# Masked cross-attention: the mask as a TensorE product ahead of the scores, the row sums as a VectorE reduction

## The reference

```python
Q = proj(q, Wq, bq); K = proj(k, Wk, bk); V = proj(v, Wv, bv)
scores = jnp.einsum('bhqd,bhkd->bhqk', Q, K) / math.sqrt(D_K)
scores = jnp.where(mask, scores, jnp.float32(-1000000000.0))   # one 128x128 mask for all
probs = jax.nn.softmax(scores, axis=-1)
attn = jnp.einsum('bhqk,bhkd->bhqd', probs, V)
```

## Time and profile before

| what | value |
|---|---|
| runs | 1013.98, 1015.27, 1017.23 us |
| span of the profiled execution, first to last instruction | 1013.6 us |
| PE busy | 946.9 us (93%) |
| PE weight loads busy | 847.0 us (84%) |
| ACT busy | 659.4 us (65%) |
| DVE busy | 635.2 us (63%) |
| POOL busy | 196.8 us (19%) |
| mean granted TensorE clock | 0.950 |
| first and last masked quad on DVE | 361.4 and 623.0 us |

### The profile page before, as it was taken

How to read it: one execution, slowest core, us unless ns; L and a number is a source line. 1 busy time by engine, 2 the same in 40 slices (tenths; PEclk the granted TensorE clock), 3 DMA queues, 4 the chain that set the end, 5 groups by cost and what they waited for, 6 DMA issues and landing times.

```text
span 1013.6 us, 19721 instructions
## 1 busy us (share of the span) xinstructions
PE 946.9 (93%) x6824; PEld 847.0 (84%) x6824; DVE 635.2 (63%) x1269; ACT 659.4 (65%) x1851; POOL 196.8 (19%) x190
## 2 busy tenths in 40 slices
PE   2899999999999899998999988999999999999997
PEld 2688989899889788877877877899999999998996
DVE  5789788788788777679787696645422342334223
ACT  3797888788888765666675576676445445444543
POOL 3112232232232432325243242100000000000000
PEclk9999999999999995788997797999999999999999
DMA  6210000000000000000100000433000000000000
GB/s 230 85 52 1 2 2 1 0 0 1 0 0 1 22 2 1 21 2 12 51 0 0 0 1 1 115 94 83 21 0 0 0 21 0 0 0 22 1 1 22
DMA packets 9998, 22.02 MB, mean 22 GB/s; under 512 B 1490, under 2 KB 1492, under 8 KB 9812
## 3 DMA queue, kind: packets, MB, share of 16 engines
q1 hardware_dynamic: 9360, 20.98, 6.5%
q10 hardware_dynamic: 580, 0.34, 0.2%
HBM read 19.21 MB, written 2.10 MB: 21 GB/s over the span
## 4 chain that ended last, share of the span: by engine, by line
PE 71%; DVE 15%; ACT 7%; issue 5%; POOL 1%; DMA 0%; DVEq 0%; ACTq 0%; POOLq 0%
PE A L414 23%; PE Y L414 21%; PE S L414 15%; PE O L414 6%; PE T L491 4%; ACT probs L695 3%; DVE nm L894 2%; DVE PT L778 2%; DVE arena L835 2%; DVE arena L915 1%; ACT arena L714 1%; DVE S L890 1%; DVE arena L922 1%; DVE xn L804 1%; ACT arena L665 1%
## 5 line engine op out<-in xcount | busy, mean ns | idle before, releaser
L778 DVE TENSOR_TENSOR PT<-probs,PT 128x512 fp32r<-128x512 f32 x128 | 88.6, 692 | 231.1 <-ACT PT L758 231.1
L414 PE MATMUL A<-XT,arena 128*128 128x512 f32 x816 | 219.1, 404 | 4.6 <-DVE arena L835 4.6
L695 ACT ACTIVATE probs<-S,nm 128x128 f32<-128x128 f32 x512 | 181.0, 369 | 47.6 <-DVE nm L894 45.9
L1111 POOL TENSOR_TENSOR probs<-probs,rinv 128x512 f32<-128x512 f32 x128 | 133.1, 1040 | 403.1 <-DVE rinv L899 403.1
L414 PEld LDWEIGHTS Y<-arena,PT 128*128 128x128 f32 x1536 | 200.3, 191 | 11.0 <-DVE PT L778 1.1
L414 PE MATMUL Y<-arena,PT 128*128 128x256 f32 x1536 | 204.0, 283 | 0.3
L414 PEld LDWEIGHTS A<-XT,arena 128*128 128x128 f32 x816 | 146.7, 192 | 35.0 <-DVE arena L835 7.3
L414 PE MATMUL O<-PT,arena 128*64 128x128 f32 (+1 forms) x1536 | 125.7, 236 | 19.9 <-DVE arena L922 9.5
L758 ACT ACTIVATE PT<-probs 128x512 fp32r<-128x512 f32 x128 | 80.8, 631 | 90.9 <-PE Y L414 90.5
L414 PEld LDWEIGHTS O<-PT,arena 128*64 128x64 f32 (+1 forms) x1536 | 112.2, 130 | 30.4 <-DVE PT L778 11.3
L414 PE MATMUL S<-arena 128*128 128x256 f32 (+1 forms) x768 | 129.3, 306 | 3.9 <-ACT probs L695 3.8
(11 more groups left out here) (96 smaller groups left out, 1065.0 us busy)
## 6 DMA issues: line engine op xcount, KB each, us to landing
wst<-in_pieces SPq DMA_DIRECT2D x52, 256.0 KB, 2.7
xs<-in_x SPq DMA_DIRECT2D x4, 512.0 KB, 4.0
craw<-in_ctxT SPq DMA_DIRECT2D x4, 512.0 KB, 3.6
out<-craw SPq DMA_DIRECT2D x4, 512.0 KB, 2.6
probs<-in_rows SPq DMA_DIRECT2D x1, 1024.0 KB, 8.1
rowc<-in_rows ACTq DMA_DIRECT2D x1, 264.0 KB
bias<-in_biases ACTq DMA_DIRECT2D x1, 37.0 KB
bkraw<-in_rows ACTq DMA_DIRECT2D x1, 2.0 KB
```

Of the source, the lines that this page charges most:

```text
L414: mm = pe.matmul(acc, lhs[a], rhs[b], start=first and i == 0, stop=last and i == 2, skip_group_check=shared)
L695: last = act.activation(probs[:, n % 4, u * P:(u + 1) * P], S[n % 2][:, u * P:(u + 1) * P], ACT.Exp, bias=nm[:, n % 4, u:u + 1], accum_out ...
L778: dve.tensor_tensor(out_, src, hi.bitcast(F32), ALU.subtract).then_inc(sem_, 1)
L1111: pool.tensor_tensor(p3, p3, rinv[:, n % 4, :].unsqueeze(2).to_broadcast([P, 4, P]), ALU.mult).then_inc(normed, 1)
```

## The change

The mask is no longer written over the scores. A constant matrix `dropped` (now fp32r, -2^60 where a key is masked, 0 elsewhere) is multiplied by an identity (`identr`, fp32r) on PE into the score bank, repeated over the four blocks by a stride of zero, and the six score matmuls accumulate onto it. On DVE the predicated copy and the wait on it are gone. In phase 1 the exponential no longer uses the accumulator; a new step `row_sum` on DVE sums the probabilities from SBUF, and the inverse waits for that sum. The hand-written order of DVE for phase 1 is another one: sum, out, inverse, probs, max instead of max, inverse, out, probs.

```diff
-MASKED = -1e9
+MASKED = -2.0 ** 60
...
-            (("max", "quad", (0, 1)), ("inverse", "quad", (1, 2)), ("out", "quad", (3, 5)),
-             ("probs", "quad", (2, 3)), ("xt1", "xt1", (0, 0)), ("residual", "residual", (4, 5)),
+            (("sum", "quad", (1, 2)), ("out", "quad", (3, 5)), ("inverse", "quad", (1, 2)),
+             ("probs", "quad", (2, 3)), ("max", "quad", (0, 1)), ("xt1", "xt1", (0, 0)), ("residual", "residual", (4, 5)),
...
                 if ph == 1:
                     pe.sem_inc(pe_gate, 1)
+                    pe.matmul(S[n % 2][:, :].rearrange("p (u c) -> p u c", u=4), identr[:, :],
+                              dropped[:, :].unsqueeze(1).to_broadcast([P, 4, P]),
+                              start=True, stop=True, skip_group_check=True)
...
                 for u in range(4):
-                    last = act.activation(probs[:, n % 4, u * P:(u + 1) * P],
-                                          S[n % 2][:, u * P:(u + 1) * P], ACT.Exp,
-                                          bias=nm[:, n % 4, u:u + 1], accum_out=rsum[:, n % 4, u:u + 1])
+                    dst, src = probs[:, n % 4, u * P:(u + 1) * P], S[n % 2][:, u * P:(u + 1) * P]
+                    if ph == 0:
+                        last = act.activation(dst, src, ACT.Exp, bias=nm[:, n % 4, u:u + 1],
+                                              accum_out=rsum[:, n % 4, u:u + 1])
+                    else:
+                        last = act.activation(dst, src, ACT.Exp, bias=nm[:, n % 4, u:u + 1])
...
-                dve.tensor_scalar(dropped[:, :], msk[:, :], 0.0, None, ALU.is_equal)
-                dve.memset(neg[:, :], MASKED)
+                dve.tensor_scalar(dropped[:, :], msk[:, :], 0.0, MASKED, ALU.is_equal, ALU.mult)
+                dve.tensor_copy(identr[:, :], ident[:, :])
...
-                if ph == 1:
-
-                    dve.sem_inc(dve_gate, 1)
-                    dve.copy_predicated(s3, dropped[:, :].unsqueeze(1).to_broadcast([P, 4, P]),
-                                        neg[:, :].unsqueeze(2).to_broadcast([P, 4, P])
-                                        ).then_inc(filled, 1)
-                    dve.wait_ge(filled, g * QUADS + n + 1)
...
+            def row_sum(ph, g, n):
+
+                if ph == 1:
+                    dve.wait_ge(exped, nth(SLOT_F2, ph, g, n))
+                    dve.tensor_reduce(rsum[:, n % 4, :],
+                                      probs[:, n % 4, :].rearrange("p (u c) -> p u c", u=4),
+                                      axis=AX.X, op=ALU.add).then_inc(summed, 1)
+
             def row_inverse(ph, g, n):
-                dve.wait_ge(exped, nth(SLOT_F2, ph, g, n))
+                if ph == 0:
+                    dve.wait_ge(exped, nth(SLOT_F2, ph, g, n))
+                else:
+                    dve.wait_ge(summed, g * QUADS + n + 1)
```

More of the change, by code:

```diff
@@ L142, in build @@
         msk = sb("msk", [P, P], U8)
-        dropped = sb("dropped", [P, P], U8)
-        neg = sb("neg", [P, 1], F32)
+        dropped = sb("dropped", [P, P], F32R)
+        identr = sb("identr", [P, P], F32R)
         half = sb("half", [P, 2], F32)
@@ L182, in build @@
         scores_ps = sem("scores_ps")
-        filled = sem("filled")
+        summed = sem("summed")
         maxed = sem("maxed")
@@ L483, in scores @@
                                [Q[rows, r, s, b * P:(b + 1) * P] for s in (0, 1)],
-                               [K[rows, r, s, b, :, :].rearrange("p h c -> p (h c)") for s in (0, 1)])
+                               [K[rows, r, s, b, :, :].rearrange("p h c -> p (h c)") for s in (0, 1)],
+                               ph == 0, True, ph == 1)
                 mm.then_inc(scores_ps, 1)
@@ L972, in _ @@
             attentions(dve, DVE_ORDER, {
-                "max": row_max, "inverse": row_inverse, "probs": probs_low, "out": out_low,
+                "max": row_max, "sum": row_sum, "inverse": row_inverse, "probs": probs_low, "out": out_low,
                 "qk": qk_low, "v": v_low, "residual": add_residual, "stats": stats,
```

## The result

The changed kernel takes 1043.88 us (median of 4 runs, 1042.07 to 1046.08) against 1014.62 us of the kernel before in the same job: 29 us more, ratio 1.0294 with a 95% interval of 1.0263 to 1.0324. The forecast was slower, at 1050 us.

A forecast was written before the change was run, and what follows sets the result against it. PE was taken to bound the cross-attention; with DVE's circle a group takes 65.3 us at full clock, 74.5 with 30 at half clock, four 298 against 263: 1015 + 35 = 1050 us, range 1012 to 1080.

The forecast's parts named there:

- a circle maximum, exponentials, sum: Cross-attention, DVE and ACT: each slot waits one round, 3.4 us, or 4.0 with the output subtraction; chance 0.55, 1050 us.
- PE bounds the stage and pays for a low clock: Cross-attention, 263 us: PE's work is 201 us at full clock; 40 us go to the low clock, 20 to waits.
- The product costs 0.24 us on PE: 64 added mask matmuls in cross-attention: 15.4 us at full clock, 19.5 with the clock mix of the kernel before.
- PE's work alone: Rival: in cross-attention the circle is hidden and only the product is paid, +19.5 us, 1035 us; chance 0.18.
- the low clock goes: Rival: earlier probabilities and more PE work end the cross-attention's half-clock stretches, faster, 1000 us; chance 0.15.
- The predicated copy for a row sum is nothing by itself: DVE in cross-attention: 0.78 us a quad goes, 0.61 comes, -11 us in all on an engine with slack.
- The order is the price: DVE's order in cross-attention: maximum last, then the same quad's sum, closes a circle longer than PE in eight slots per group.
- My formula: Cross-attention group time: h + (1 - h/94) x 65.3 = 65.3 + 0.305 h us, h being its half-clock time.
- 54.0 + 5: Cross-attention group at full clock without the circle: PE's own work with the product, 54.0 us, plus 5 us idle.
- h, the time at half clock: PE's half-clock time per cross-attention group: 23.7 us before, taken as 30 after because more idle brings more falls.
- the stage's clock would be 0.80 or less: Sign to look for: the cross-attention's clock, 0.82 before, is 0.80 or less in the profile after.
- The wait ahead of the row sum: Sign on DVE: waits for ACT's exponentials of about 1 us in bare slots, near 40 us in the stage.

The follow-up runs named there:

- product_old_order: The kernel before with the PE product in place of the predicated copy; accumulator and DVE order (max, inverse, out, probs) as before: 986.95 us, ratio 0.9726.
- sum_old_order: The changed kernel with DVE's order max, sum, inverse, out, probs: 994.02 us, ratio 0.9764.
- copy_gone: The kernel before without the predicated copy, the mask left out and nothing in its place: 992.87 us, ratio 0.9802.
- sum_alone: The kernel before with the row sum for the accumulator, predicated copy kept, no product, order max, sum, inverse, out, probs: 1051.53 us, ratio 1.0316.
- product_alone: The kernel before with the PE product added and the predicated copy kept as well: 1005.27 us, ratio 0.9888.
- accum_new_order: The changed kernel, maximum still last on DVE, with the accumulator and no row sum: 1049.91 us, ratio 1.0322.
- product_only: The changed kernel with the maximum first on DVE (output ahead of inverse), the accumulator again and no row sum: 994.92 us, ratio 0.9796.
- max_first: The changed kernel with the maximum first on DVE (max, sum, out, inverse, probs): 1007.33 us, ratio 0.9912.
- no_product: The changed kernel without the mask product, the mask left out altogether: 1043.33 us, ratio 1.0267.
- order_alone: The kernel before with only DVE's order changed (inverse, out, probs, max), predicated copy and accumulator kept: 1094.77 us, ratio 1.0779.

## Why the prediction was right, and where it was not

The time, the sign and the mechanism came as forecast: +29 us against +35, and a circle maximum, exponentials, sum on DVE and ACT. That the total came so close is in part luck, because wrong terms cancelled. Point by point:

- *PE bounds the stage and pays for a low clock.* Right. The stages of the two fastest kernels are at a clock of 0.99 and 0.96. In product_old_order PE is busy for 227 of 236 us with 5 us at half clock, so its work is about 225 us, where I had counted 54.0 x 4 = 216.
- *The product costs 0.24 us on PE.* Right as a time from start to start between running matmuls (0.23; behind a wait 0.40), wrong as a price. I added 15.4 to 19.5 us to the total for it. Added alone it takes 11 us away, since the half-clock time falls from 95 to 35 us; taken out of the changed kernel it changes nothing. The rival "PE's work alone" (1035 us) is refuted by both. My rival "the low clock goes" (1000 us) is what the same kernel does without the new order: sum_old_order takes 994 us, with 24 us at half clock.
- *The predicated copy for a row sum is nothing by itself, since DVE has slack.* This is a step that failed. The copy's removal alone is worth 20 us (copy_gone), the row sum alone costs 32 (sum_alone). They are of one length and I set them off against each other, -0.17 us a quad. In the order of the kernel before, with the product, the swap is worth 1.2%: sum_old_order 0.9764 against product_alone 0.9888, at nearly equal DVE work (200 and 205 us). With product_old_order between the two (0.9726), the copy's removal gives 1.6% and the sum in place of the accumulator costs 0.4%, within the intervals. The copy stood ahead of the maximum, and so of the exponentials; the sum stands behind them, with only POOL's step waiting. That this is why the two are not worth the same is argued, not tried.
- *The order is the price.* Right, and too small. My formula gave 65.3 us a group against 54.0 + 5 without the circle, 25 us in all at full clock. Measured are 54 us with the product and the sum (sum_old_order to the changed kernel), 53 for the maximum's place with product and accumulator (accum_new_order against product_only), 79 in the kernel before. Of the 54, 39 are the maximum's place. They fit the formula once the clock is put in: 71.5 us a group with the changed kernel's 20.4 us at half clock (next point) against 8.9 + (1 - 8.9/94) x 59 = 62.3 for max_first, 37 us in four groups. The order brings back the waits before PE, and with them the stretches at half clock. The other 15 us are the output ahead of the inverse, a term that I had put at nothing. The clock makes 4 of them (61.3 us a group for sum_old_order), and PE idles 18 us in place of 11; the rest stays open.
- *h, the time at half clock, taken as 30 us a group.* This size was wrong: measured 20.4 (81 / 4), less than before the change, where I had argued for more. My formula with 20.4 gives 65.3 + 0.305 x 20.4 = 71.5 us a group and 286 for the stage, against 291 measured. The forecast that the stage's clock would be 0.80 or less is a miss (0.86).
- *The wait ahead of the row sum, about 40 us in all.* 34.2 us in 36 pieces, up to 1.2 us. Right.

So the change is one loss of 54 us, DVE's order, laid over a gain of 24 us that the other edits bring by themselves. That the clock is higher with the product is shown by three pairs of kernels: 0.82 and 0.93 (before, product_alone), 0.75 and 0.86 (no_product, changed), 0.92 and 0.99 (copy_gone, product_old_order). Whether it is so by its activity or because it shifts the waits is open: the runs do not separate it.

The prediction drew on the Trainium skill (TensorE: Matmul & The Clock Gate, "A second HAM failure mode: psum-queue depth-cycling") for short idle between groups of matmuls that makes the clock swing. The runs agree: PE's work in the stage is 50 or 54 us a group in all these kernels by my count, and the time at half clock goes from 5 to 205 us, with no wait of PE longer than 2.6 us (order_alone). By an estimate from the table of the Trainium skill (VectorE: DVE Perf Modes, the section on the TRN2 errata) a reduction from SBUF takes 594 ns, 64 ns less than one from PSUM, and the section says itself that this row comes out too short. 0.69 us for the sum from SBUF and 0.68 for the maximum from PSUM were measured, and the measurement decides.

## What to carry to other kernels

In an engine's hand-written order, look for a step and, one slot later, the step that needs its answer through one other engine. The two close a circle, and its length is a floor for every slot (here 3.28 us, 4.24 with the output), whatever the engines' shares of busy time say. Price a removed and an added instruction of equal length apart, by what waits behind each. Where the matmul engine's clock falls behind short waits, as it does here, a little more work on it can cost nothing or less than nothing, and a wait can cost more than its length.

## What the runs showed that I had not expected

Sixty-four additional matmuls made the kernel before 1.1% faster (0.9888, interval 0.9845 to 0.9931), with nothing taken off any engine.

The four operations that apply LayerNorm on DVE took 1.99 us in one group of the changed kernel (485.02 to 487.01, first row) and 2.73 us in the kernel before, for the same shape and count. In the kernel before POOL was at work over the first 1.9 us of them (last two rows), in the changed kernel over the first 0.9 us. The trace of the changed kernel has 48 such operations: the 43 with no POOL operation beside them take 394 to 412 ns, the five that overlap one take 701 to 1825. That POOL's work stretches them is read from this; no run varied it.

```profile
485.02 1.99 DVE L795 TENSOR_SCALAR xn<-xs,mv,rstd 128x256 f32 x4
```

And in the kernel before:

```profile
472.65 2.73 DVE L804 TENSOR_SCALAR xn<-xs,mv,rstd 128x256 f32 x4
...
472.26 1.04 POOL L1111 TENSOR_TENSOR probs<-probs,rinv 128x512 f32<-128x512 f32 x1
473.26 1.32 POOL L1144 TENSOR_TENSOR CT<-craw,CT 128x512 fp32r<-128x512 f32 x1
```
